# A fused conditioning and mixture-of-experts kernel on one core: the order of VectorE's work in the first group, and of TensorE's products and VectorE's weighing in the second

## The chip, the cores and the metric

The kernel runs on one core of a Trainium2 chip. The metric is the device time of one execution in microseconds (us), and less is better. Beside each timed execution one was profiled: its trace gives every instruction's start and length on TensorE (PE for the products, PEld for the loads of the stationary operand), VectorE (DVE), ScalarE (ACT), GpSimd (POOL) and the queue of SyncE (SP), which issues most transfers.

## What is computed

The reference, cut to what matters (64 batches of 64 rows, so 4096 rows of 512; 6 experts of rank 16):

```python
q_emb = relu(cond @ W3 + b3)
x1 = (64 * x + sum(x, axis=1)) * q_emb[:, None, :]
y = relu(x1 @ W2 + b2)
gates = softmax(y @ W_router + b_router)
w = the gates of the two best experts, zero elsewhere
h = y @ A_r            # per expert, and y @ A_s shared
out = x + y @ W_base + b_base + (y @ A_s) @ B_s + sum_e (w_e * h_e) @ B_r[e]
```

Each float32 factor is split into a rounded part (`hi`) and a rest (`lo`), and a product is three products of TensorE: hi with hi, hi with lo, lo with hi.

## The kernel before

The 4096 rows are eight groups of 512 tokens. A group's work has these parts:

- **x.** The four pieces `c` of 128 features come transposed. VectorE turns a piece (`turn_x`, `turn`), sums it per batch and adds (`sum_x` and `add_sum`, together `total`), GpSimd scales it by `qT` (`scale`, L308), ScalarE rounds it to `x1_hi` (`x1_split`, L347, in the step called `split`), and VectorE takes the rest `x1_lo` (`x1_rest`, L491, in the step called `rest`). The pieces of group g + 1 are made while group g is multiplied.
- **m1.** y's four tiles `m` of 128 features, each a sum over the four pieces: 12 products a tile, 48 in all. Tiles 0, 1 and 2 have PSUM banks of their own. Tile 3 has the bank of `m2_ps[2]`, so it begins only when VectorE has read the output tile 2 of the group before (`add_x`, L625).
- **relu.** For each tile ScalarE writes `y_hi` (L353), and then the full value back to the bank (L355). VectorE takes the rest `y_lo` (`y_rest`, L497).
- **h and m2.** 12 products of y with the narrow weights give `hT` (`h`), and 48 with `W_base` give the output tiles (`m2`).
- **Routing.** ScalarE copies `hT` to `h_head` (L441), VectorE ranks the experts and makes the gates (L544 to L583, `rank_experts` and `gates`), and SP spreads the gates to `gatesT` by four DMAs (L263). In the next group's step VectorE weighs h (`weigh`, L598), ScalarE rounds it (`hw_split`, L415), VectorE takes its rest (`hw_rest`, L611), and TensorE adds 12 products to the output tiles that stand in PSUM (`up`, in the order 2, 0, 1, 3). Then `add_x` adds x to each tile and SP stores it.

There is no scheduler. Each engine runs a list written out by hand, in its own order, and waits on semaphores. TensorE's order in a group but the first is: m1 of tiles 0 to 2, `up` for the group before, m1 of tile 3, three of the four parts of `h`, six products of `m2`, the last part of `h`, and the other 42 products of `m2`. That is 120 products a group. The wait ahead of m1 of tile 3 is this line, and `UP_TILES[:1]` is output tile 2:

```python
if m == KC - 1:
    pe.wait_ge(out_ready, TT * (g - 1) + 1)
```

The first group differs. Its x is turned by TensorE (`head_ps`), `h` and `m2` of output tile 0 alternate, and there is no `up`. The second group's step on VectorE is the branch `elif second`, and the products of its m1 are in the loop `m1(g, par, m)`, tile by tile, with a wait for `x1_lo` of piece k ahead of the three products of piece k. Products with zeros (`keep_warm`, L724) fill TensorE's time at the start. VectorE's time, for the x of group g + 1 and for y of group g, is one queue, so whatever stands ahead of an instruction there delays it.

Of the kernel before, what the change touches and what calls it, by code (L numbers as in the profile page):

```python
# [22 lines left out]
def adaln_ffn(nc, x, cond, W3, b3, W2, b2, W_base, b_base, A_s, B_s, A_r, B_r, W_router, b_router, out):  # L23
# [6 lines left out]
    P = 128  # L30
# [3 lines left out]
    KC = D // P  # L34
    QC = Q // P
    TG = 512
# [11 lines left out]

    WARM_LOAD, WARM_W3, WARM_HALF, WARM_Q = 7, 1, 2, 1
    assert ONE < SH and SH + R <= RO and RO + E * R == P and TT == KC and NG % 2 == 0 and NG >= 4  # L50
# [6 lines left out]
    with ctx:  # L57
# [277 lines left out]
        def _(act):  # L335
# [43 lines left out]

            q_relu(0)  # L380
            W2_split(0)
            q_relu(1)
            x1_split_head(0)
            q_relu(2)
            x1_split_head(1)
            q_relu(3)
            W2_split(1)
# [31 lines left out]
            def step(g, par):  # L419
                first, second, last = place(g)  # L420

                def split(c):
                    if not last:
                        x1_split(g + 1, 1 - par, c)

                for m in range(KC):
                    relu(g, m, first)
                    if m == 0 and not first:
                        hw_split(slice(0, TG), g)
                    if not first and m >= (2 if second else 1):  # L430
                        split(m - (2 if second else 1))
                if first:
                    act.wait_ge(Wu_loaded, 48)
                    nc.scalar.activation(Wu_hi[:, :], Wu_f[:, :], ACT.Copy).then_inc(Wu_hi_ready, 1)
                    pick_round()

# [8 lines left out]
                if first:  # L445
                    split(0)
                    split(1)
# [16 lines left out]
        def _(dve):  # L464
# [163 lines left out]
            def step(g, par):  # L628
# [20 lines left out]

                if first:  # L650
                    turn(0)
                    total(0)
                    y_rest(g, 0)
                    turn(1)
                    y_rest(g, 1)
                    sum_x(g + 1, 1)
                    y_rest(g, 2)
                    add_sum(g + 1, 1)
                    y_rest(g, 3)
                    turn(2)  # L660
                    total(2)
                elif second:
                    y_rest(g, 0)
                    weigh_before()
                    turn(0)
                    total(0)
                    hw_rest_before()
                    y_rest(g, 1)
# [31 lines left out]
                if first:  # L700
                    rest(0)
                if first or second:
                    turn(3)
                    total(3)
                if first:
                    rest(1)
                rest(2)
# [12 lines left out]
        def _(pe):  # L720
# [50 lines left out]
            def m1_first():  # L771
# [5 lines left out]

                for k in range(KC // 2):
                    pe.wait_ge(x1_hi_ready, k + 1)
                    pe.wait_ge(W2_hi_ready, k + 1)  # L780
                    for m in range(KC):
                        if k == 0:
                            pe.wait_ge(qT_ready, m + 1)
                        chunk(m, k, W2_hi, x1_hi)
                    pe.wait_ge(W2_lo_ready, k + 1)
                    for m in range(KC):
                        chunk(m, k, W2_lo, x1_hi)
                    pe.wait_ge(x1_lo_ready, k + 1)
                    for m in range(KC):
                        chunk(m, k, W2_hi, x1_lo)  # L790
                for tiles in ((0, 1), (2, 3)):
                    for k in range(KC // 2, KC):
                        pe.wait_ge(x1_hi_ready, k + 1)
                        pe.wait_ge(W2_lo_ready, k + 1)
                        for m in tiles:
# [4 lines left out]
                            if k == KC - 1:  # L800
                                last.then_inc(m1_done, 1)

            def h(g, k, first):
# [52 lines left out]
            def step(g, par):  # L856
                first, second, last = place(g)
                if first:
                    m1_first()
                else:  # L860
                    for m in range(KC - 1):
                        m1(g, par, m)
                    up(UP_TILES, g)
                    m1(g, par, KC - 1)
# [57 lines left out]
```

## Time and profile before

| what | value |
|---|---|
| time, median of 3 runs | 237.69 us (237.68 to 237.79) |
| time of the profiled execution | 237.04 us |
| its span, first to last instruction | 235.2 us |
| TensorE busy with products | 229.3 us (97%), 1006 products |
| VectorE busy | 166.7 us (71%) |
| ScalarE busy | 86.2 us (37%) |
| GpSimd busy | 49.0 us (21%) |

A product's record lasts 0.39 us, but the records overlap: products are pipelined, so it is the distance from one start to the next that counts. A start that comes later than that distance after the start ahead of it is time that TensorE stood still.

### The profile page before, as it was taken

Reading aid. Unit: us, or ns where it says so; the run is one execution under the profiler, and the core shown is the slowest. Engines: PE = TensorE matmul, PEld = TensorE weight load, DVE = VectorE, ACT = ScalarE, POOL = GpSimd, SP = SyncE. Lnnn points to the kernel's source line nnn. Section 1 sums busy time; section 2 is a strip of 40 time slices with the busy share of each in tenths; the row PEclk is TensorE's granted clock in tenths of the full one; section 3 lists DMA queues with packets and bytes.
Section 4 is the critical chain, followed back from the end, with each engine's and each line's share of the span. In section 5 each row is a group of like instructions: output and inputs, shape, how many; then the busy total and the mean of one; then the engine's idle time right before and its main releaser. Section 6 shows DMA issues by size and latency. Waiting matters only on the chain.

```text
span 235.2 us, 3088 instructions
## 1 busy us (share of the span) xinstructions
PE 229.3 (97%) x1006; PEld 186.9 (79%) x1006; DVE 166.7 (71%) x309; ACT 86.2 (37%) x171; POOL 49.0 (21%) x57
## 2 busy tenths in 40 slices
PE   7999899999999999999999999999999999999994
PEld 3977687788888888888888888888888888888883
DVE  0794997798979967497838969299665976064344
ACT  3369451534136330444206340263305351252330
POOL 6288422012132211023012120022111130000000
PEclk9999999999999999999999999999999999999999
DMA  6999903527053632717044541709020370104004
GB/s 214 340 219 227 253 4 71 142 99 261 11 137 65 222 137 37 175 70 289 8 117 89 187 172 22 185 4 329 28 33 0 126 231 13 22 0 178 3 0 178
DMA packets 32505, 28.80 MB, mean 122 GB/s; under 512 B 5817, under 2 KB 22909, under 8 KB 32494
## 3 DMA queue, kind: packets, MB, share of 16 engines
q1 hardware_dynamic: 30682, 28.50, 42.4%
q10 hardware_dynamic: 1812, 0.17, 0.6%
q8 instruction: 6, 0.10, 0.2%
q14 instruction: 5, 0.04, 0.1%
HBM read 18.89 MB, written 8.39 MB: 116 GB/s over the span
## 4 chain that ended last, share of the span: by engine, by line
PE 87%; SPq 6%; DVE 2%; DMA 2%; issue 0%; DVEq 0%
PE m_ps L747 78%; PE hT L747 9%; SPq L210 3%; DMA x_quart<-in_x_dram 2%; DVE out_nat L625 1%; SPq L226 1%; SPq L233 1%; SPq L229 1%; DVE xT L471 0%; SPq L231 0%; DVE vsum L476 0%; DVE x_sum L483 0%; SPq L237 0%; DVE y_lo L497 0%; SPq L236 0%
## 5 line engine op out<-in xcount | busy, mean ns | idle before, releaser
L308 POOL TENSOR_TENSOR x_full<-x_sum,qT 128x512 f32<-128x512 f32 x28 | 32.4, 1156 | 136.7 <-DVE x_sum L483 136.7
L353 ACT ACTIVATE y_hi<-m_ps,condT 128x512 fp32r<-128x512 f32 x32 | 21.9, 686 | 80.4 <-PE m_ps L747 80.2
L747 PE MATMUL m_ps<-Wb_lo,y_hi 128*128 128x512 f32 x128 | 49.8, 389 | 0.0
L747 PE MATMUL m_ps<-Wb_hi,y_hi 128*128 128x512 f32 x128 | 49.8, 389 | 0.0
L747 PE MATMUL m_ps<-Wb_hi,y_lo 128*128 128x512 f32 x128 | 49.8, 389 | 0.0
L747 PE MATMUL m_ps<-x_hi,W_hi 128*128 128x512 f32 x112 | 43.8, 391 | 0.0
L747 PE MATMUL m_ps<-x_hi,W_lo 128*128 128x512 f32 x112 | 43.6, 389 | 0.0
L747 PE MATMUL m_ps<-x_lo,W_hi 128*128 128x512 f32 x112 | 43.6, 389 | 0.0
L497 DVE TENSOR_TENSOR y_lo<-m_ps,y_hi 128x512 fp32r<-128x512 f32 x32 | 21.7, 677 | 30.3 <-ACT m_ps L355 30.3
L471 DVE STREAM_TRANSPOSE xT<-x_quart 128x512 f32<-128x512 f32 x28 | 30.3, 1084 | 3.0 <-DMA x_quart<-in_x_dram 3.0
L747 PEld LDWEIGHTS m_ps<-Wb_hi,y_lo 128*128 128x128 f32 x128 | 24.0, 188 | 5.0
L747 PEld LDWEIGHTS m_ps<-Wb_hi,y_hi 128*128 128x128 f32 x128 | 24.0, 188 | 4.9
L747 PEld LDWEIGHTS m_ps<-Wb_lo,y_hi 128*128 128x128 f32 x128 | 24.0, 188 | 4.9
L747 PEld LDWEIGHTS m_ps<-x_hi,W_hi 128*128 128x128 f32 x112 | 21.0, 188 | 5.0 <-DVE x_lo L491 0.7
L747 PEld LDWEIGHTS m_ps<-x_hi,W_lo 128*128 128x128 f32 x112 | 21.0, 188 | 4.4
L747 PEld LDWEIGHTS m_ps<-x_lo,W_hi 128*128 128x128 f32 x112 | 21.0, 188 | 4.2
L347 ACT ACTIVATE x_hi<-x_full 128x512 fp32r<-128x512 f32 x28 | 17.5, 628 | 17.7 <-POOL x_full L308 17.7
L625 DVE TENSOR_TENSOR out_nat<-m_ps,x_nat 128x512 f32<-128x512 f32 x32 | 20.4, 679 | 2.1 <-PE m_ps L747 2.1
L491 DVE TENSOR_TENSOR x_lo<-x_full,x_hi 128x512 fp32r<-128x512 f32 x28 | 19.3, 707 | 2.5 <-ACT x_hi L347 2.4
L355 ACT ACTIVATE m_ps<-m_ps,condT 128x512 f32<-128x512 f32 x32 | 20.9, 653 | 0.0
L483 DVE SCALAR_TENSOR_TENSOR x_sum<-xT,vsum 128x512 f32<-128x512 f32 x28 | 19.4, 692 | 2.1
L476 DVE TENSOR_REDUCE vsum<-xT 128x8 f32<-128x512 f32 x28 | 19.0, 680 | 0.4
(99 smaller groups left out, 255.1 us busy)
## 6 DMA issues: line engine op xcount, KB each, us to landing
out_dram<-out_nat SPq DMA_DIRECT2D x32, 256.0 KB, 2.3
x_quart<-in_x_dram SPq DMA_DIRECT2D x28, 256.0 KB, 4.5
x_nat<-in_x_dram SPq DMA_DIRECT2D x7, 1024.0 KB, 6.2
gatesT<-wT SPq DMA_DIRECT2D x28, 48.0 KB
x_nat<-in_x_dram SPq DMA_DIRECT2D x4, 256.0 KB, 3.4
W_f<-in_L_cond_W_dram SPq DMA_DIRECT2D x4, 256.0 KB, 6.0
Wb_f<-in_L_ffn_W_base_dram SPq DMA_DIRECT2D x1, 1024.0 KB, 8.7
W_sb<-in_L_cond_W_dram SPq DMA_DIRECT2D x2, 256.0 KB, 4.2
```

The costliest lines, as they stand in the source:

```text
L210: eng.dma_start(Wd_f[:, k, RO:P].rearrange("p (e r) -> p e r", r=R), A_r[:, k * P:(k + 1) * P, :].rearrange("e p r -> p e r")).then_inc(Wd ...
L308: nc.gpsimd.tensor_tensor(per_batch(x1_full[:, c, :]), per_batch(x1_sum[:, c, :]), qT[:, c, bass.ds(BG * g, BG)].unsqueeze(2).to_broadcast ...
L347: nc.scalar.activation(x1_hi[par][:, c, :], x1_full[:, c, :], ACT.Copy).then_inc(x1_hi_ready, 1)
L353: nc.scalar.activation(y_hi[:, m, :], m1_ps[m][:, :], ACT.Relu, bias=b2_sb[:, m:m + 1]).then_inc(y_hi_ready, 1)
L355: nc.scalar.activation(m1_ps[m][:, :], m1_ps[m][:, :], ACT.Relu, bias=b2_sb[:, m:m + 1]).then_inc(y_full_ready, 1)
L471: nc.vector.transpose(xT[c % 2][:, :], x_quart[par][:, :, :].rearrange("p b (i c) -> p c b i", c=KC)[:, c]).then_inc(xT_ready, 1)
L476: nc.vector.tensor_reduce(vsum[c % 2][:, :], per_batch(xT[c % 2][:, :]), AX.X, ALU.add).then_inc(vsum_ready, 1)
L483: nc.vector.scalar_tensor_tensor(out=per_batch(x1_sum[:, c, :]), in0=per_batch(xT[c % 2][:, :]), scalar=float(N), in1=vsum[c % 2][:, :].un ...
L491: nc.vector.tensor_tensor(x1_lo[par][:, c, :], x1_full[:, c, :], x1_hi[par][:, c, :].bitcast(F32), ALU.subtract).then_inc(x1_lo_ready, 1)
L497: nc.vector.tensor_tensor(y_lo[:, m, :], m1_ps[m][:, :], y_hi[:, m, :].bitcast(F32), ALU.subtract).then_inc(y_lo_ready, 1)
L625: nc.vector.tensor_tensor(out_nat[par][:, t, :], m2_ps[t][:, :], x_nat[par][:, t, :], ALU.add).then_inc(out_ready, 1)
L747: mm = nc.tensor.matmul(psum, lhsT, rhs, start=start and i == 0, stop=stop and i == len(terms) - 1)
```

## The change

Four places are edited. The values and the number of instructions are the same, but for one product with zeros less.

1. **Head.** `WARM_HALF` goes from 2 to 1. ScalarE rounds each `q_relu` one place earlier. In the first group's m1, piece 0, tile 3's two products with `x1_hi` go behind those of tiles 0 to 2, so that the wait for the last `qT` comes later.
2. **First group, VectorE.** Each `y_rest` goes ahead of the piece of x that stood before it. `turn(2)` and `total(2)` go behind the gates, and the first `rest` behind `total(3)`. ScalarE takes `split(0)` ahead of the copy of `hT`, and the four copies called `pick_round` go to the second group.
3. **Second group, TensorE.** m1 of tiles 0 to 2 takes the 24 products with `x1_hi`, piece by piece over the three tiles, and then the 12 with `x1_lo`, tile by tile (`m1_second`).
4. **Second group, VectorE and ScalarE.** `weigh` and `hw_rest` go ahead of all `y_rest`, and `hw_split` ahead of all `relu`.

```diff
-    WARM_LOAD, WARM_W3, WARM_HALF, WARM_Q = 7, 1, 2, 1
+    WARM_LOAD, WARM_W3, WARM_HALF, WARM_Q = 7, 1, 1, 1
...
             q_relu(0)
+            q_relu(1)
             W2_split(0)
-            q_relu(1)
+            q_relu(2)
             x1_split_head(0)
-            q_relu(2)
+            q_relu(3)
             x1_split_head(1)
-            q_relu(3)
             W2_split(1)
...
+                if second:
+                    hw_split(slice(0, TG), g)
                 for m in range(KC):
                     relu(g, m, first)
-                    if m == 0 and not first:
+                    if m == 0 and not first and not second:
                         hw_split(slice(0, TG), g)
...
                     nc.scalar.activation(Wu_hi[:, :], Wu_f[:, :], ACT.Copy).then_inc(Wu_hi_ready, 1)
+                    split(0)
+                if second:
                     pick_round()
...
                 if first:
-                    split(0)
                     split(1)
...
                 if first:
+                    y_rest(g, 0)
+                    turn(0)
+                    y_rest(g, 1)
+                    total(0)
+                    y_rest(g, 2)
+                    turn(1)
+                    y_rest(g, 3)
+                    total(1)
+                elif second:
+                    weigh_before()
+                    hw_rest_before()
+                    y_rest(g, 0)
                     turn(0)
                     total(0)
...
-                elif second:
-                    y_rest(g, 0)
-                    weigh_before()
-                    turn(0)
-                    total(0)
-                    hw_rest_before()
                     y_rest(g, 1)
                     turn(1)
                     add_x(g - 1, 1 - par, UP_TILES[:1], 0)
...
                 if first:
-                    rest(0)
+                    turn(2)
+                    total(2)
                 if first or second:
                     turn(3)
                     total(3)
                 if first:
+                    rest(0)
                     rest(1)
...
+            def m1_second():
+
+                x_hi, x_lo = x1_hi[1], x1_lo[1]
+                for k in range(KC):
+                    pe.wait_ge(x1_hi_ready, KC + k + 1)
+                    for m in range(KC - 1):
+                        cols = slice(m * P, (m + 1) * P)
+                        product(m1_ps[m][:, :], [(W2_hi[:, k, cols], x_hi[:, k, :]),
+                                                 (W2_lo[:, k, cols], x_hi[:, k, :])], k == 0, False)
+                for m in range(KC - 1):
+                    cols = slice(m * P, (m + 1) * P)
+                    for k in range(KC):
+                        if m == 0:
+                            pe.wait_ge(x1_lo_ready, KC + k + 1)
+                        mm = product(m1_ps[m][:, :], [(W2_hi[:, k, cols], x_lo[:, k, :])], False, k == KC - 1)
+                    mm.then_inc(m1_done, 1)
...
-                    for m in range(KC - 1):
+                    if second:
+                        m1_second()
+                    for m in () if second else range(KC - 1):
                         m1(g, par, m)
```

The first place is VectorE from the last rest of the head to the ranking, in the first group. `xT`, `vsum` and `x_sum` belong to the x of the second group, `y_lo` to the y of the first. Before:

```order
L523 TENSOR_TENSOR x_lo<-hT,x_hi 128x512
L471 STREAM_TRANSPOSE xT<-x_quart 128x512
L476 TENSOR_REDUCE vsum<-xT 128x8
L483 SCALAR_TENSOR_TENSOR x_sum<-xT,vsum 128x512
L497 TENSOR_TENSOR y_lo<-m_ps,y_hi 128x512
L471 STREAM_TRANSPOSE xT<-x_quart 128x512
L497 TENSOR_TENSOR y_lo<-m_ps,y_hi 128x512
L476 TENSOR_REDUCE vsum<-xT 128x8
L497 TENSOR_TENSOR y_lo<-m_ps,y_hi 128x512
L483 SCALAR_TENSOR_TENSOR x_sum<-xT,vsum 128x512
L497 TENSOR_TENSOR y_lo<-m_ps,y_hi 128x512
```

The same stretch of VectorE in the changed kernel:

```order
L526 TENSOR_TENSOR x_lo<-hT,x_hi 128x512
L500 TENSOR_TENSOR y_lo<-m_ps,y_hi 128x512
L474 STREAM_TRANSPOSE xT<-x_quart 128x512
L500 TENSOR_TENSOR y_lo<-m_ps,y_hi 128x512
L479 TENSOR_REDUCE vsum<-xT 128x8
L486 SCALAR_TENSOR_TENSOR x_sum<-xT,vsum 128x512
L500 TENSOR_TENSOR y_lo<-m_ps,y_hi 128x512
L474 STREAM_TRANSPOSE xT<-x_quart 128x512
L500 TENSOR_TENSOR y_lo<-m_ps,y_hi 128x512
L479 TENSOR_REDUCE vsum<-xT 128x8
L486 SCALAR_TENSOR_TENSOR x_sum<-xT,vsum 128x512
```

The first `y_lo` moved ahead of three instructions on x, and the last one from behind two turns and a whole sum to behind two turns and the first piece's sum.

The second place is the second group: TensorE's products of m1, with buffer numbers. Before, from the last three of tile 0 (`m1_ps0`) to the first of tile 1:

```order
L747 MATMUL m1_ps0<-x1_hi1,W2_hi 128x512
L747 MATMUL m1_ps0<-x1_lo1,W2_hi 128x512
L747 MATMUL m1_ps0<-x1_hi1,W2_lo 128x512
L747 MATMUL m1_ps1<-x1_hi1,W2_hi 128x512
L747 MATMUL m1_ps1<-x1_lo1,W2_hi 128x512
```

The same place of TensorE in the changed kernel, the last piece's products with `x1_hi` and all with `x1_lo`, up to the first product of `up` (`Wu_hi`):

```order
L749 MATMUL m1_ps0<-x1_hi1,W2_hi 128x512
L749 MATMUL m1_ps0<-x1_hi1,W2_lo 128x512
L749 MATMUL m1_ps1<-x1_hi1,W2_hi 128x512
L749 MATMUL m1_ps1<-x1_hi1,W2_lo 128x512
L749 MATMUL m1_ps2<-x1_hi1,W2_hi 128x512
L749 MATMUL m1_ps2<-x1_hi1,W2_lo 128x512
L749 MATMUL m1_ps0<-x1_lo1,W2_hi 128x512 x4
L749 MATMUL m1_ps1<-x1_lo1,W2_hi 128x512 x4
L749 MATMUL m1_ps2<-x1_lo1,W2_hi 128x512 x4
L749 MATMUL m2_ps2<-Wu_hi,hw_hi 128x512
```

Tile 0's last product was the 12th of the group, and is now the 28th; tile 1's went from the 24th to the 32nd, and tile 2's stays the 36th. `up` follows as the 37th in both.

VectorE in the same group, from the first `y_lo` to the first addition of x (`out_nat`), before:

```order
L497 TENSOR_TENSOR y_lo<-m_ps,y_hi 128x512
L598 SCALAR_TENSOR_TENSOR hw_full<-hT,h_bias,gatesT 128x512
L471 STREAM_TRANSPOSE xT<-x_quart 128x512
L476 TENSOR_REDUCE vsum<-xT 128x8
L483 SCALAR_TENSOR_TENSOR x_sum<-xT,vsum 128x512
L611 TENSOR_TENSOR hw_lo<-hw_full,hw_hi 128x512
L497 TENSOR_TENSOR y_lo<-m_ps,y_hi 128x512
L471 STREAM_TRANSPOSE xT<-x_quart 128x512
L625 TENSOR_TENSOR out_nat<-m_ps,x_nat 128x512
```

And in the changed kernel:

```order
L601 SCALAR_TENSOR_TENSOR hw_full<-hT,h_bias,gatesT 128x512
L614 TENSOR_TENSOR hw_lo<-hw_full,hw_hi 128x512
L500 TENSOR_TENSOR y_lo<-m_ps,y_hi 128x512
L474 STREAM_TRANSPOSE xT<-x_quart 128x512
L479 TENSOR_REDUCE vsum<-xT 128x8
L486 SCALAR_TENSOR_TENSOR x_sum<-xT,vsum 128x512
L500 TENSOR_TENSOR y_lo<-m_ps,y_hi 128x512
L474 STREAM_TRANSPOSE xT<-x_quart 128x512
L628 TENSOR_TENSOR out_nat<-m_ps,x_nat 128x512
```

`hw_full` and `hw_lo` left the stretch between the first `y_lo` and `out_nat` and stand ahead of it; the first `y_lo`, the first piece of x, the second `y_lo` and a turn still stand ahead of `out_nat`.

The third place is ScalarE in the head, the difference between the two (`qT` is `q_relu`, `W_hi` is `W2_split`, `x_hi` is `x1_split_head`):

```order
-L367 ACTIVATE qT<-m_ps,b_sb 128x64
+L367 ACTIVATE qT<-m_ps,b_sb 128x64 x2
 L373 ACTIVATE W_hi<-W_f 128x512
 L367 ACTIVATE qT<-m_ps,b_sb 128x64
```

Two `qT` now stand ahead of the first `W_hi`, and so three ahead of the first `x_hi`, where there were two.

## Rows read from the trace of the kernel before

**Rows 1.** The page: TensorE's granted clock in 40 slices, tenths of full speed.

```profile
PEclk9999999999999999999999999999999999999999
```

**Rows 2.** Chain that ended last, one later group: start, length (us), what.

```profile
83.49 23.12 PE m_ps L747 x102
```

**Rows 3.** Timeline of the head: start, length, what, idle before.

```profile
8.52 0.59 PE L724 MATMUL m_ps<-idle 128*128 128x512 bf16 x2
8.95 1.40 PE L766 MATMUL m_ps<-condT,W_sb 128*128 128x64 f32 x6
...
9.52 0.31 ACT L367 ACTIVATE qT<-m_ps,b_sb 128x64 f32<-128x64 f32 x1 [4.09 <-PE m_ps L766]
9.73 0.62 ACT L373 ACTIVATE W_hi<-W_f 128x512 fp32r<-128x512 f32 x1
...
10.26 0.31 ACT L367 ACTIVATE qT<-m_ps,b_sb 128x64 f32<-128x64 f32 x1
...
10.60 0.60 ACT L378 ACTIVATE x_hi<-m_ps 128x512 fp32r<-128x512 f32 x1
...
11.25 1.43 PE L774 MATMUL m_ps<-x_hi,W_hi 128*128 128x512 f32 x4
...
17.43 0.19 PEld L774 LDWEIGHTS m_ps<-x_lo,W_hi 128*128 128x128 f32 x1 [0.17 <-DVE x_lo L523]
```

**Rows 4.** Timeline of the first group: y of it, x of the second.

```profile
20.02 0.65 ACT L355 ACTIVATE m_ps<-m_ps,condT 128x512 f32<-128x512 f32 x1
...
21.15 1.10 DVE L471 STREAM_TRANSPOSE xT<-x_quart 128x512 f32<-128x512 f32 x1 [3.01 <-DMA x_quart<-in_x_dram]
...
22.55 0.39 PE L747 MATMUL hT<-y_hi,Wd_hi 128*128 128x512 f32 x1
...
23.62 0.68 DVE L497 TENSOR_TENSOR y_lo<-m_ps,y_hi 128x512 fp32r<-128x512 f32 x1
...
24.22 1.10 DVE L471 STREAM_TRANSPOSE xT<-x_quart 128x512 f32<-128x512 f32 x1
24.36 0.50 PE L747 MATMUL hT<-y_lo,Wd_hi 128*128 128x512 f32 x1 [1.19 <-DVE y_lo L497]
29.23 1.50 ACT L441 ACTIVATE h_head<-hT,h_bias 32x128 f32<-32x128 f32 x4 [3.05 <-PE hT L747]
```

**Rows 5.** Timeline of the second group: TensorE, ScalarE and GpSimd.

```profile
37.33 1.43 POOL L308 TENSOR_TENSOR x_full<-x_sum,qT 128x512 f32<-128x512 f32 x1 [5.46 <-DVE x_sum L483]
...
37.87 0.39 PE L747 MATMUL m_ps<-x_hi,W_hi 128*128 128x512 f32 x1
38.78 0.63 ACT L347 ACTIVATE x_hi<-x_full 128x512 fp32r<-128x512 f32 x1 [6.10 <-POOL x_full L308]
40.76 0.40 PE L747 MATMUL m_ps<-x_hi,W_lo 128*128 128x512 f32 x1
41.20 0.69 ACT L353 ACTIVATE y_hi<-m_ps,condT 128x512 fp32r<-128x512 f32 x1 [1.78 <-PE m_ps L747]
41.78 0.65 ACT L355 ACTIVATE m_ps<-m_ps,condT 128x512 f32<-128x512 f32 x1
49.33 0.39 PE L747 MATMUL m_ps<-x_hi,W_hi 128*128 128x512 f32 x1
```

**Rows 6.** Timeline of the second group: VectorE, and SP's issues of `gatesT`.

```profile
34.26 3.88 SPq L263 DMA_DIRECT2D gatesT<-wT  x4
42.47 0.69 DVE L497 TENSOR_TENSOR y_lo<-m_ps,y_hi 128x512 fp32r<-128x512 f32 x1 [2.33 <-ACT m_ps L355]
43.08 0.74 DVE L598 SCALAR_TENSOR_TENSOR hw_full<-hT,h_bias,gatesT 128x512 f32<-128x512 f32 x1
43.73 1.09 DVE L471 STREAM_TRANSPOSE xT<-x_quart 128x512 f32<-128x512 f32 x1
...
46.19 0.68 DVE L611 TENSOR_TENSOR hw_lo<-hw_full,hw_hi 128x512 fp32r<-128x512 f32 x1
...
48.41 0.65 DVE L625 TENSOR_TENSOR out_nat<-m_ps,x_nat 128x512 f32<-128x512 f32 x1
```

More of the change, by code:

```diff
@@ L650, in step @@
                 if first:
+                    y_rest(g, 0)
[10 more added lines that the diff above has]
+                    y_rest(g, 0)
                     turn(0)
                     total(0)
-                    y_rest(g, 0)
[L654 to L661, printed above, removed]
-                elif second:
-                    y_rest(g, 0)
-                    weigh_before()
-                    turn(0)
-                    total(0)
-                    hw_rest_before()
                     y_rest(g, 1)
@@ L776, in chunk @@
                                             stop=k == KC - 1 and x1 is x1_lo)
-                for k in range(KC // 2):
+                pe.wait_ge(x1_hi_ready, 1)
+                pe.wait_ge(W2_hi_ready, 1)
+                for m in range(KC - 1):
+                    pe.wait_ge(qT_ready, m + 1)
+                    chunk(m, 0, W2_hi, x1_hi)
+                pe.wait_ge(W2_lo_ready, 1)
+                for m in range(KC - 1):
+                    chunk(m, 0, W2_lo, x1_hi)
+                pe.wait_ge(qT_ready, KC)
+                chunk(KC - 1, 0, W2_hi, x1_hi)
+                chunk(KC - 1, 0, W2_lo, x1_hi)
+                pe.wait_ge(x1_lo_ready, 1)
+                for m in range(KC):
+                    chunk(m, 0, W2_hi, x1_lo)
+                for k in range(1, KC // 2):
                     pe.wait_ge(x1_hi_ready, k + 1)
@@ L781, in m1_first @@
                     for m in range(KC):
-                        if k == 0:
-                            pe.wait_ge(qT_ready, m + 1)
                         chunk(m, k, W2_hi, x1_hi)
@@ L801, in m1_first @@
                                 last.then_inc(m1_done, 1)
+            def m1_second():
+                x_hi, x_lo = x1_hi[1], x1_lo[1]
+                for k in range(KC):
+                    pe.wait_ge(x1_hi_ready, KC + k + 1)
+                    for m in range(KC - 1):
+                        cols = slice(m * P, (m + 1) * P)
+                        product(m1_ps[m][:, :], [(W2_hi[:, k, cols], x_hi[:, k, :]),
+                                                 (W2_lo[:, k, cols], x_hi[:, k, :])], k == 0, False)
+                for m in range(KC - 1):
+                    cols = slice(m * P, (m + 1) * P)
[4 more added lines that the diff above has]
+                    mm.then_inc(m1_done, 1)
             def h(g, k, first):
```

## The prediction

> **What bounds the kernel now.** I read the page first: TensorE is busy 97% of the span, at full clock in every slice [rows 1]. So the time is TensorE's products at their distance, plus the places where it stands still. The chain that ended last gives the distance: 102 products in 23.12 us, 0.227 us each [rows 2]. With it I went through TensorE's timeline. From 42 us to the end each start follows the last by that distance, so nothing on another engine costs time there. The still times are all ahead of 50 us, and the change works on them:
>
> - In the first group `h` starts at 22.55, and its third product should start at 23.00. It starts at 24.36, because VectorE turned and summed a piece of x from 21.15 on and reached the first `y_lo` only at 23.62 [rows 4]. With restarts after short waits, the 60 products from 22.55 to 37.87 take 15.32 us, where 60 distances are 13.60: 1.72 us lost [rows 4, 5].
> - In the second group, from 37.87 to the start of m1's tile 3 at 49.33, 48 products take 11.46 us, where 48 distances are 10.88: 0.58 us lost, in short waits for `x_lo` and `hw_lo` [rows 5].
>
> These 2.3 us are what the change can win. To know what it wins I walk the new order with the lengths of the old rows.
>
> **Part by part: the head.** One product with zeros less lets the last `q` products start 0.21 us earlier (two took 0.59 us, and one record is 0.38) [rows 3]. The first `q_relu` moves from 9.52 to 9.31. The second tile's sum follows the first: six products in 1.40 us, the last one 0.40 long, are 0.20 apart, two for a tile, so the second `q_relu` starts at 9.71. Then comes `W2_split` 0.21 later (as 9.52 to 9.73), at 9.92, the third `q_relu` 0.53 later (as 9.73 to 10.26), at 10.45, and the first `x_hi` 0.21 to 0.34 later (9.52 to 9.73, 10.26 to 10.60), at 10.66 to 10.79, where it was 10.60 [rows 3]. I take 10.70: the first product of m1 0.1 us later than before. The later wait for `qT` gives TensorE 0.25 us back: its first four products took 0.93 us from start to start where 0.34 + 2 x 0.23 = 0.80 would do, and it restarted once more for 0.11 us. But at 17.43 TensorE waited for an `x_lo` [rows 3]. That one ends an unbroken line of work on VectorE, which starts from the first `x_hi`, and so comes 0.1 us later too. **Head: +0.1 us.** Its ends are -0.2 (all of the 0.21 kept) and +0.3 (the `x_hi` at 10.79, and 0.1 for another wait).
>
> **First group.** `h` starts at 22.65. The first full y is there at 20.02 + 0.1 + 0.65 = 20.77 [rows 4], when VectorE still waits for the x transfer (to 21.15), so the first `y_lo` takes time that was idle: 20.8 to 21.5. After it VectorE runs without a break: `y_lo` 0.60 to its successor (23.62 to 24.22), a turn 1.0, `y_lo` 0.60, sum and addition 1.33 (43.73 to 46.19 is 2.46 with the turn's 1.13), `y_lo` 0.60, a turn 1.0, and the fourth `y_lo` 0.68 [rows 4, 6]. It ends at 26.65. TensorE wants it for the 21st product, at 22.65 + 20 x 0.227 = 27.18, and the others with more to spare. So the 60 products run at their distance, and the second group starts at 22.65 + 13.60 = **36.25 us, 1.62 earlier than 37.87**.
>
> **Second group, m1 and x.** Is its x there? `hT` is complete 1.62 earlier, so its copy starts at 27.61 instead of 29.23 [rows 4]. From that copy to SP's first issue of `gatesT` were 5.03 us (29.23 to 34.26) [rows 4, 6]; as much at most gives 32.65. Two turns and sums follow (2 x 2.46), to 37.6, then GpSimd's scaling (1.43) and ScalarE's rounding (0.63) [rows 5]: the fourth `x_hi` is there at 39.75 with 0.1 for the handing over. Before it was there at 39.41, and so this is about as late as it was, but the new order wants it only at the 19th product, 36.25 + 18 x 0.227 = 40.33. The fourth `x_lo` is there at 40.5, and wanted by the 28th, at 42.37. No wait is left, with 0.6 us to spare. The weighing now stands ahead of `y_lo` on VectorE and could block it: SP's four issues end 1.6 earlier, at 36.5, and `weigh` at 43.08 did not wait for a landing 4.9 us behind its last issue at 38.14 [rows 6], so the gates are there by 41.5 at the latest. 0.74 + 0.63 + 0.68 for `hw_full`, `hw_hi` and `hw_lo` end by 43.7, ahead of `up` (36.25 + 36 x 0.227 = 44.41) and of the first full y. **The 0.58 us are won too: -2.2 us by the end of `up`,** at 36.25 + 10.88 = 47.13.
>
> **What is late next.** m1 of tile 3 needs its bank, which VectorE frees by the first `out_nat`. Before, that ended at 48.41 + 0.65 = 49.06, and TensorE came at 49.33 [rows 5, 6]: 0.27 us ahead. It stands behind the second group's first `y_lo`, a turn, a sum, the second `y_lo` and another turn. The first `y_lo` needs tile 0 of m1 complete, and by `m1_second` that is no longer the 12th product but the 28th. It starts at 42.37. Then ScalarE: `y_hi` 0.44 later (40.76 to 41.20), L355 another 0.58 (41.20 to 41.78), 0.65 long [rows 5]: 44.04, and VectorE's `y_lo` at 44.08. Before it started at 42.47 [rows 6]. **So it comes 1.6 us later, though m1 starts 1.6 us earlier.** From its start to the end of `out_nat` were 6.59 us (42.47 to 49.06). `hw_full` and `hw_lo` leave that stretch: 0.65 (43.08 to 43.73) and 0.60 less [rows 6], 5.34 us. `out_nat` ends at 49.42. TensorE's load starts 0.06 later (24.30 to 24.36), at 49.48, and a restart costs 0.1 (the record of 24.36 is 0.50 long, not 0.39) [rows 4]: as if at 49.58. Before: 49.33.
>
> **Sum.** -1.62 (first group, with the head's +0.1 in it), -0.58 (second group's waits), +2.45 (a new wait of 2.35 us, and a restart), together **+0.25 us**. All later work on TensorE moves by that; VectorE's line, 0.36 later at `out_nat`, reaches the x of the third group before it is wanted. The profiled execution's 237.04 us become 237.3. It was 0.65 under the median of the runs, so 237.69 becomes **237.9 us**. What the first edits save is saved on TensorE ahead of a point whose time VectorE sets. Each tenth that m1 of the second group starts sooner still moves that point, since the chain hangs on its start; the order of the products costs 16 x 0.227 = 3.6 us on it.
>
> **Rivals.**
>
> - *The saving is kept* (6 in 100). If m1 of tile 3 did not wait, everything would move by -1.62 - 0.58 = -2.2: 235.5 us. For it speaks that two operations of VectorE leave the stretch, 1.25 us; against it that 0.27 us was all there was to spare, and that 1.6 + 2.2 us are to be made up. A shorter line on VectorE, by 0.7 us, would already be faster by over 0.2%: 2 in 100.
> - *Slower: VectorE's line to `out_nat` is longer than I sum it.* I have +0.25, and +0.48 is the bound of 0.2%, so 0.23 us decide. The head's +0.3 instead of +0.1 gives 238.1; a late piece of x in the second group, past its 0.6 us to spare, or `hw_lo` in front of the first `y_lo`, past 0.3, adds what it is late by. Two such tenths give 238.3 to 238.5. 14 in 100.
> - *Slower: the clock.* TensorE would stand still for 2.35 us, longer than the 1.2 us at 24.36, through which the clock stayed at full [rows 1, 4]. If it fell to the lower of its two levels, half of the upper, the twelve products of tile 3 would take 0.227 us more each: +2.7, 240.6 us. The Trainium skill ("TensorE: Matmul & The Clock Gate", Part 1: The HAM clock gate) says that the throttled state is the default and that activity releases it, which speaks for such a fall; the trace shows none after any still time of before. 4 in 100.
>
> **How the numbers follow.** 0.2%, 0.48 us, is about what a measurement of this kernel can tell from no change. My forecast, the saving given back at m1 of tile 3, has the rest, 74 in 100. Its own bounds are the head's (-0.3 to +0.2 about my value), the chain's (0.1 either way) and the spread of the runs (0.1): 237.5 to 238.3. With the slower line the range is 237.4 to 238.5, and leaves out the kept saving, the clock and the ends of the rest, under 2 in 10. Faster 8 in 100, within 0.2% 74, slower 18.
>
> **What would show it.** Right: no wait of TensorE for `y_lo` in the first group; the second group's first product near 36.3; no waits in its m1; then a wait of TensorE for `out_nat` of 2.3 us near 47.1 to 49.5, which the trace of before has nowhere; the first `y_lo` of the second group near 44.1. Wrong in the head: the first `x_hi` at 10.5 or earlier, or after 10.8. It would be wrong as a whole if m1 of tile 3 starts near 47.2, if a clock below 1.00 stands behind the wait, or if TensorE waits again after 52 us.

## The result, and the profile after

| | before | changed |
|---|---|---|
| median of 6 runs | 237.69 us (236.98 to 237.79) | 240.64 us (238.99 to 242.09) |
| ratio to before, 95% interval | | 1.0129 (1.0081 to 1.0177) |
| granted clock of the executions, mean | 0.997 to 1.000 in all 91 timed beside the later experiments | 0.993 in two, 0.986 in four |
| profiled execution: time, span | 237.04, 235.2 us | 242.09, 240.1 us |

The kernel became 2.95 us slower, outside the range of 237.4 to 238.5 us. Its times are also spread over 3 us, where before they lay within 1. The page of the changed kernel shows two slices in which TensorE was granted less than its full clock, where before there was none [rows 1]:

```profile
span 240.1 us, 3086 instructions
PEclk9979999997999999999999999999999999999999
```

The view of TensorE's loads and whom they waited for has the forecast wait, and no wait for `y_lo` or for the second group's `x_lo` any more (columns: us in total, times, longest):

```profile
PEld m_ps L749 <- DVE out_nat L628: 2.6, 1, 2.6
...
PEld m_ps L776 <- ACT x_hi L378: 0.3, 1, 0.3
```

The timeline of the same execution: the first product of the head's m1, and then from `h` of the first group to m1's tile 3 of the second. It answers to [rows 3 to 6]:

```profile
13.25 1.65 PE L776 MATMUL m_ps<-x_hi,W_hi 128*128 128x512 f32 x3
...
25.68 0.39 PE L749 MATMUL hT<-y_hi,Wd_hi 128*128 128x512 f32 x1
...
26.13 0.39 PE L749 MATMUL hT<-y_lo,Wd_hi 128*128 128x512 f32 x1
...
39.28 0.39 PE L749 MATMUL m_ps<-x_hi,W_hi 128*128 128x512 f32 x1
...
44.72 2.88 PE L749 MATMUL m_ps<-x_lo,W_hi 128*128 128x512 f32 x12
...
45.83 0.69 ACT L353 ACTIVATE y_hi<-m_ps,condT 128x512 fp32r<-128x512 f32 x1 [0.66 <-PE m_ps L749]
...
47.10 0.69 DVE L500 TENSOR_TENSOR y_lo<-m_ps,y_hi 128x512 fp32r<-128x512 f32 x1 [1.20 <-ACT m_ps L355]
...
51.75 0.65 DVE L628 TENSOR_TENSOR out_nat<-m_ps,x_nat 128x512 f32<-128x512 f32 x1
...
52.45 0.50 PE L749 MATMUL m_ps<-x_hi,W_hi 128*128 128x512 f32 x1 [2.14 <-DVE out_nat L628]
...
53.98 0.63 PE L749 MATMUL m_ps<-x_hi,W_hi 128*128 128x512 f32 x1
...
56.55 0.63 PE L749 MATMUL hT<-y_hi,Wd_hi 128*128 128x512 f32 x1
```

Three things are to be seen. From `h` to the second group the 60 products take 13.60 us (25.68 to 39.28), their distance and nothing more. m1's tile 3 starts 13.17 us after m1 itself, where the walk had 13.23. And both stand 3.1 us late: `h` starts at 25.68, where before it was 22.55 [rows 4]. The head lost that, and in two places: its first product of m1 starts 2.0 us later than before (13.25, before 11.25 [rows 3]), and from there to `h` are 12.43 us, where before they were 11.30. Behind the wait the products' records grow from 0.39 to 0.63 us and their distance from 0.227 to 0.43.

The windows view gives the granted clock of such stretches, the number behind the five engines' busy times. The windows of 1 us show how low it goes, the longer ones its surroundings:

```profile
12.50:15.00 2.50, 2.35 (x7) 1.91 (x7) 2.15 (x4) 2.47 (x7) 1.73 (x2) 0.59 1.21 188
13.00:14.00 1.00, 0.85 (x3) 0.66 (x3) 0.77 (x2) 1.00 (x4) 0.85 (x1) 0.50 1.39 193
15.00:20.00 5.00, 5.00 (x20) 4.02 (x20) 4.68 (x8) 2.82 (x6) 4.62 (x4) 0.86 1.08 223
...
48.00:52.00 4.00, 2.32 (x11) 1.58 (x9) 3.93 (x6) 1.79 (x4) 1.04 (x1) 1.00 0.00 0
52.00:56.00 4.00, 3.54 (x11) 2.86 (x12) 3.97 (x7) 0.21 (x1) 0.00 (x0) 0.74 0.33 126
54.00:55.00 1.00, 1.00 (x4) 0.81 (x3) 1.00 (x3) 0.00 (x0) 0.00 (x0) 0.50 0.33 127
56.00:60.00 4.00, 4.00 (x16) 3.17 (x16) 2.65 (x5) 2.89 (x7) 1.25 (x1) 0.84 0.95 309
```

The clock is lower twice: in the head, when the first group's m1 has just begun, and behind the wait. In both it goes to 0.50, the lower of its two levels, 1.2 instead of 2.4 GHz. Ahead of the first fall TensorE did narrow products of `q` with one product with zeros less among them, ahead of the second it stood still. From 53.72 to 57.37 nine distances take 3.65 us, where 9 x 0.227 are 2.04: that fall cost 1.6 us. The other fall is the 1.1 us that the way to `h` grew by.

A third stretch is not in the clock row. The head's transposes of x, before any edit takes effect, ran at two speeds. The view of the tile `hT`, from 4 to 10 us, lists its four transposes (shortest, median, longest in ns, first and last start); in the changed kernel's profile:

```profile
L739 PE MATMUL hT<-ident,x_nat x4: 421/421/421, 6.0 to 8.6; 128*128 128x128 f32 x4
```

In the profile of before:

```profile
L737 PE MATMUL hT<-ident,x_nat x4: 283/283/284, 5.5 to 6.9; 128*128 128x128 f32 x4
```

So the profile of before, on which the walk was built, had a quick head, and this one a slow head from its first products on. Whether that is of the change had to be asked too. A start like the one of before, with the first `q` product at 7.28 us, is called an early start below; in this profile it comes at 9.24, a late start.

### The profile page after: what moved, and what is told of

Same layout as the page of the kernel before. It is cut to its first block, busy times and chain, and to the rows that moved or that the text cites. A ratio compares the mean times of both kernels' runs of the same rounds, so it can differ in the third digit from the quotient of the medians.

```text
span 240.1 us, 3086 instructions
## 1 busy us (share of the span) xinstructions
PE 233.0 (97%) x1005; PEld 191.1 (80%) x1005; DVE 166.2 (69%) x309; ACT 86.4 (36%) x171; POOL 48.8 (20%) x57
## 4 chain that ended last, share of the span: by engine, by line
PE 94%; DVE 2%; DMA 1%; ACT 1%; issue 1%; ACTq 0%; DVEq 0%
PE m_ps L749 77%; PE hT L749 9%; PE m_ps L776 5%; DMA cond_sb<-in_L_cond_b_dram 1%; DVE out_nat L628 1%; PE m_ps L739 1%; PE m_ps L768 1%; DVE xT L474 0%; PE hT L739 0%; PE m_ps L726 0%; ACTq L336 0%; ACT qT L367 0%; ACT W_hi L373 0%; ACT x_hi L378 0%; PE m_ps L732 0%
## 5 line engine op out<-in xcount | busy, mean ns | idle before, releaser
L749 PE MATMUL m_ps<-x_hi,W_lo 128*128 128x512 f32 x112 | 44.1, 394 | 0.0
L749 PE MATMUL m_ps<-x_lo,W_hi 128*128 128x512 f32 x112 | 42.3, 393 | 0.0
```

The source lines that it names most:

```text
L749: mm = nc.tensor.matmul(psum, lhsT, rhs, start=start and i == 0, stop=stop and i == len(terms) - 1)
```

## The experiments

All were timed over 5 rounds beside the kernel before. "Clock" is the mean granted clock of an execution, listed for each. One low stretch makes 0.993 (or 0.990 to 0.992) of it, two make 0.986.

**e1: the product with zeros back.**

```diff
-    WARM_LOAD, WARM_W3, WARM_HALF, WARM_Q = 7, 1, 1, 1
+    WARM_LOAD, WARM_W3, WARM_HALF, WARM_Q = 7, 1, 2, 1
```

> The changed kernel with WARM_HALF back at 2, all else as changed. Theory A (the low clock of the head, 13.0 to 16.4 us, comes of the product with zeros that was taken out): only the low clock behind the wait for out_nat is left in every execution, mean granted clock 0.993, 238.9 to 239.6 us. Theory B (it comes of the other edits of the head, or of a chance in how early the clock rises at the start): 0.986 in about as many executions as in the changed kernel, 4 in 6, and the median stays near 240.6 us.

Measured: 239.30 us (237.42 to 240.04, 9 runs), ratio 1.0057 (1.0037 to 1.0078). No execution at 0.986: four at 0.993 (239.30 to 240.04) and five at 1.000 (237.42 to 239.31). Theory A holds for the head: the execution with two low stretches is gone. It was wrong in one thing, that the fall behind the wait comes in every execution: it comes in four of nine. The profiled execution is one without it, with an early start, and so the one that the prediction walked through. Its timeline:

```profile
36.49 0.39 PE L749 MATMUL m_ps<-x_hi,W_hi 128*128 128x512 f32 x1
...
44.31 0.69 DVE L500 TENSOR_TENSOR y_lo<-m_ps,y_hi 128x512 fp32r<-128x512 f32 x1 [1.19 <-ACT m_ps L355]
...
48.97 0.65 DVE L628 TENSOR_TENSOR out_nat<-m_ps,x_nat 128x512 f32<-128x512 f32 x1
...
49.67 0.50 PE L749 MATMUL m_ps<-x_hi,W_hi 128*128 128x512 f32 x1 [2.14 <-DVE out_nat L628]
```

Forecast were 36.25, 44.08, an end of `out_nat` at 49.42 (here 49.62) and 49.48. The execution took 237.42 us, and 237.3 was forecast for one like the profile of before.

**e2: the head's edits alone, on the kernel before** (`WARM_HALF` 1, the order of `q_relu`, the order of piece 0 in the first group's m1).

> The kernel before with the edits of the head alone (WARM_HALF 1, ScalarE's and TensorE's new order). Theory A: the low clock of the head is there in some executions, 0.993 in those, 1.000 in the others, and the time is bimodal, 237.7 and about 239.3 us. Rival (the head is innocent, both low stretches belong to the groups): 1.000 always and 237.5 to 237.9 us.

Measured: 237.81 us (237.31 to 238.46, 12 runs), ratio 1.0002 (0.9993 to 1.0012). The clock is 0.990 or 0.993 in ten of twelve executions, and between 0.997 and 1.000 in all 32 of the kernel before beside them. So the head's edits make the clock fall, and the time doesn't move: neither expectation had that. Executions at 0.993 average 237.73 us, the two without a fall 238.00. In the profiled one the clock is low from 12 to 14 us, and `h` starts 1.7 us later than in the profile of before. The low clock has 0.9 us of that (from the first product of m1 to `h` are 12.23 us, where 11.30 were), and a later start the rest:

```profile
12.00:14.00 2.00, 1.96 (x5) 1.58 (x6) 1.95 (x3) 1.80 (x4) 1.30 (x2) 0.50 1.14 347
```

```profile
L747 PE MATMUL hT<-y_hi,Wd_hi x4: 389/392/395, 24.3 to 29.3; 128*128 128x512 f32 x4
L747 PE MATMUL hT<-y_lo,Wd_hi x4: 389/444/502, 25.3 to 29.8; 128*128 128x512 f32 x4
```

The first `y_lo` product follows at 25.3, where before it was 24.36. Of 1.7 us of lateness 0.8 was hidden in the wait for `y_lo` here.

**e3: the changed kernel, with ten products with zeros in the wait for `out_nat`.**

```diff
                     up(UP_TILES, g)
+                    if second:
+                        for _ in range(10):
+                            nc.tensor.matmul(hT[:, :], idle[:, 0:P], idle[:, :], start=True, stop=True)
```

> The changed kernel with ten products with zeros on TensorE (into the bank of hT, which is free there) ahead of the wait for out_nat in the second group. The wait stays, 2.3 us, but TensorE is at work in it. Theory (the clock falls because TensorE stands still there, and that costs 1.7 us on top of the wait): no low clock at 54 to 57 us, and the time is 1.5 to 1.7 us less than the changed kernel's, 237.9 us where the head keeps its clock and 239.3 to 240.4 where it doesn't. Rival (the low clock has another cause, or the wait alone costs the time): no gain, 240.6 us.

Measured: 239.00 us (237.66 to 240.42, 12 runs), ratio 1.0050 (1.0031 to 1.0069), 1.6 us less than the changed kernel. The lowest clock is 0.992, in five of twelve: the second fall is gone. The two ranges that were expected, with and without the head's fall, are not what came. The seven without it lie at 237.66 to 238.03 (three) and 239.10 to 239.41 (four), the five with it at 238.56 to 239.06 and once at 240.42. So there are two heaps 1.4 us apart, and the head's fall adds about 1 us to either. The waits of its loads have 0.5 us left for `out_nat`:

```profile
PEld m_ps L749 <- DVE out_nat L628: 0.5, 1, 0.5
```

The windows behind it are at full clock, where the head's 12 to 14 us are not:

```profile
12.00:14.00 2.00, 2.00 (x6) 1.52 (x6) 1.86 (x4) 1.42 (x3) 1.30 (x2) 0.50 1.18 324
...
54.00:56.00 2.00, 2.00 (x10) 1.66 (x9) 1.67 (x3) 1.09 (x3) 1.25 (x1) 1.00 1.01 379
```

**e4: `add_x` of output tile 2 early.** VectorE's order in the second group of the changed kernel:

```diff
                     weigh_before()
+                    turn(0)
                     hw_rest_before()
+                    total(0)
                     y_rest(g, 0)
-                    turn(0)
-                    total(0)
                     y_rest(g, 1)
-                    turn(1)
                     add_x(g - 1, 1 - par, UP_TILES[:1], 0)
+                    turn(1)
```

> The changed kernel with VectorE's order in the second group weigh, turn(0), hw_rest, total(0), y_rest 0, y_rest 1, add_x of output tile 2, turn(1). Theory (VectorE's line to out_nat gives the saving back): TensorE waits no more ahead of m1 of tile 3, no low clock behind it, and 237.69 - 2.2 = 235.5 us where the head keeps its clock, 237.0 to 238.0 where it doesn't. Rival (the wait is set by something else, as the products of up or a late piece of x): a wait of over 1 us stays, and over 238 us.

Measured: 237.12 us (235.64 to 238.18, 12 runs), ratio 0.9982 (0.9959 to 1.0004). The wait for `out_nat` is gone from TensorE's waits. The clock is 0.990 or 0.993 in nine of twelve; that this is the head's fall is shown by e5, not by this run's profile, which has none. 3.5 us less than the changed kernel, and that includes the fall behind the wait. Without it the profiles give 2.2 us: from the second group's m1 to the end are 197.0 us here and 199.2 in e1. So the line on VectorE is what gave the saving back. The edit shortens that line in two ways, which were not separated: `turn(1)` leaves it, and `turn(0)` and `total(0)` go ahead of the first `y_rest`.

**e5: e4 with `WARM_HALF` 2.**

> As e4, with WARM_HALF back at 2. Theory A (the low clock of the head comes of the product taken out, and each us that the head is late is now a us of the kernel): no low clock anywhere, 235.5 us where the clock rises early at the start and about 236.9 where it rises late; median under 236.5, below e4's 237.12. Theory B (the spread of e4 has another cause): as e4, 237.1 us.

Measured: 236.28 us (235.61 to 237.19, 7 runs), ratio 0.9946 (0.9922 to 0.9969). All executions at 0.998 to 1.000, as theory A had it. The times lie in two heaps, 235.61 to 236.28 (four) and 237.06 to 237.19 (three). VectorE's `out_nat` ends at 47.68 in its profile, and TensorE starts tile 3 at 48.29 without a wait:

```profile
23.81 0.39 PE L749 MATMUL hT<-y_hi,Wd_hi 128*128 128x512 f32 x1
...
47.00 0.68 DVE L628 TENSOR_TENSOR out_nat<-m_ps,x_nat 128x512 f32<-128x512 f32 x1
...
48.29 0.39 PE L749 MATMUL m_ps<-x_hi,W_hi 128*128 128x512 f32 x1
```

**e6: the first group's edits alone, on the kernel before.**

> The kernel before with the first group's edits alone (each y_rest ahead, turn(2) and total(2) behind the gates, ScalarE's split(0) ahead and pick_round in the second group). Theory: h runs without a wait, and m1 of the second group starts 1.6 us earlier, but tile by tile it wants x_lo of the fourth piece at its 12th product, 38.6 us, and has it at 40.4: the saving goes into that wait. 237.5 to 237.9 us, more where the clock falls behind it. Rival (the first group's saving is kept without the second group's edits): 236.1 us.

Measured: 238.83 us (238.11 to 240.20, 8 runs), ratio 1.0051 (1.0029 to 1.0073). Slower than either expectation. The saving does go into waits for `x_lo`, two of them, the first of 2.1 us already at the first piece, since its `rest` now stands behind `total(3)`:

```profile
39.94 0.47 PE L747 MATMUL m_ps<-x_hi,W_hi 128*128 128x512 f32 x1 [1.92 <-DVE x_lo L492]
...
41.30 0.50 PE L747 MATMUL m_ps<-x_hi,W_hi 128*128 128x512 f32 x1 [0.43 <-DVE x_lo L492]
```

One of the eight executions is at 0.992. So each half of the change needs the other: this one needs `m1_second`, which asks for `x_lo` late.

**e7: the second group's edits alone, on the kernel before.**

> The kernel before with the second group's edits alone (m1_second, weigh and hw_rest ahead of y_rest, hw_split ahead of relu). Theory (tile 0 done 16 products later sets out_nat): m1 starts at 37.9 as before, out_nat ends 1.6 us later, a wait of 2.3 us; 239.5 us where the clock keeps its level, 240.9 to 241.2 where it falls behind the wait. Rival (the wait costs only what the first group's edits saved): 237.7 us.

Measured: 239.55 us (239.44 to 241.58, 6 runs), ratio 1.0106 (1.0073 to 1.0139). Four executions at 1.000, 239.44 to 239.60, and two at 0.993, 241.26 and 241.58. The sizes are about as the theory had them: +1.9 us for tile 0 done 16 products later, and 1.9 more where the clock falls behind the wait, of which 1.4 to 1.7 were expected. The timeline:

```profile
46.42 0.69 DVE L499 TENSOR_TENSOR y_lo<-m_ps,y_hi 128x512 fp32r<-128x512 f32 x1 [1.99 <-ACT m_ps L355]
...
51.08 0.64 DVE L627 TENSOR_TENSOR out_nat<-m_ps,x_nat 128x512 f32<-128x512 f32 x1
...
51.78 0.50 PE L749 MATMUL m_ps<-x_hi,W_hi 128*128 128x512 f32 x1 [2.14 <-DVE out_nat L627]
```

**e8 and e9: the same lateness put into two kernels,** the kernel before (e8) and e5 (e9): six products with zeros more behind the first `q` products, 1.27 us.

```diff
-                keep_warm(WARM_HALF if k == 0 else WARM_Q)
+                keep_warm(WARM_HALF + 6 if k == 0 else WARM_Q)
```

> The kernel before with six products with zeros more in the head, behind the first q products: all of the head 1.27 us later. Theory (the x transfer and the pieces of x, not TensorE, set the third product of h there, so a late head is hidden in its wait): under 0.3 us on the median, 237.7 to 238.0 us. Rival (the head is on the path): 239.0 us.

> e5 with the same six products with zeros more in the head as e8. Theory (with each y_rest ahead, the first group's h waits for nothing, and a late head is a late kernel): the full 1.27 us on e5's 236.28, 237.3 to 237.8 us, where the same edit cost the kernel before 0.4 us. Rival (the head is hidden here too): under 236.8 us.

Measured: e8 238.10 us (237.56 to 238.39, 12 runs), ratio 1.0010 (0.9999 to 1.0021), +0.4 us, a little over the 0.3 expected. e9 238.19 us (236.92 to 238.70, 12 runs), ratio 0.9999 (0.9979 to 1.0020). Its median is 1.9 us over e5's, more than the 1.27 us put in, but both kernels have two heaps, and the median changed heaps. Heap by heap, the means went from 235.91 (four of e5) to 237.17 (five of e9) and from 237.13 (three) to 238.41 (seven): +1.26 and +1.28 us, the lateness put in and nothing else. So before, two thirds of such lateness are hidden, and in the new order of the first group nothing is. e8's profile, which has the late start as well, shows how the kernel before hides it. VectorE's head ends at 21.33, and the turn of x follows at 21.25, 0.1 us later than before [rows 4]; `h` starts at 25.73, 3.2 us later than before, and its `y_lo` product at 26.18 without a wait:

```profile
20.64 0.69 DVE L523 TENSOR_TENSOR x_lo<-hT,x_hi 128x512 fp32r<-128x512 f32 x1
21.25 1.12 DVE L471 STREAM_TRANSPOSE xT<-x_quart 128x512 f32<-128x512 f32 x1
...
24.24 0.68 DVE L497 TENSOR_TENSOR y_lo<-m_ps,y_hi 128x512 fp32r<-128x512 f32 x1
...
25.73 0.39 PE L747 MATMUL hT<-y_hi,Wd_hi 128*128 128x512 f32 x1
...
26.18 0.39 PE L747 MATMUL hT<-y_lo,Wd_hi 128*128 128x512 f32 x1
```

That execution's span is 236.3 us, 1.1 more than that of before, for 3.2 us of lateness.

**e10: e5 with an eighth product with zeros at the start** (`WARM_LOAD` 8).

> e5 with an eighth product with zeros ahead of the transposes. Theory (the records' two speeds of the transposes, 0.28 and 0.42 us each, are the clock's rise at the start, which falls early or late): if more work in front makes the early rise more frequent, the median goes from 236.28 towards 235.7 and the spread shrinks. Rival (the time of the rise is not set by it): 236.3 to 236.5 us, spread as before.

Measured: 236.31 us (235.87 to 236.61, 6 runs), ratio 0.9927 (0.9902 to 0.9952). The spread shrank to 0.74 us and the median did not move: the first as the theory had it, the second as its rival. In its profile the transposes of `hT` have both lengths (283/309/418 ns, shortest, median, longest), so if the two lengths are two levels of the clock, the rise fell among them.

**e11: e3 with `WARM_HALF` 2,** so both causes of a low clock are gone and the wait is left.

> The changed kernel with both causes of low clock taken away: WARM_HALF 2 and the ten products in the wait for out_nat. Theory (what is left is the saving given back at out_nat, plus the late start where the clock rises late): clock 1.000 in every execution, 237.4 us with an early rise and about 238.8 with a late one. Rival (there is a further loss): a low clock or over 239.2 us.

Measured: 239.14 us (238.18 to 239.51, 11 runs), ratio 1.0041 (1.0022 to 1.0060), all executions at 0.999 or 1.000. The times are in two heaps, 238.18 to 238.51 (five) and 239.14 to 239.51 (six). The lower heap is 0.9 us above the 237.4 expected. Its profiled execution (238.37 us) shows why: it has the quick transposes, but among them TensorE waited 0.2 us for the last of x's four transfers. Its first `q` product starts at 7.86 where e1's starts at 7.36, and `h` at 23.58 where e1's is at 22.89. So a start can be late in two ways. In e5's profile this wait is the longest:

```profile
7.35 0.63 PE L739 MATMUL m_ps<-ident,x_nat 128*128 128x128 f32 x3 [0.50 <-DMA x_nat<-in_x_dram]
```

That the upper heap is the slow transposes is likely, but not shown: it wants a profile of each execution.

**e12: e5 with the whole head of before.**

> e5 with the head of before altogether, ScalarE's and TensorE's order too. Theory of the prediction (the new order of the head costs 0.1 us at the first x_hi): 0.1 us less than e5, 235.9 to 236.4 us. Rival (the later wait for the last qT gives TensorE 0.25 us back): 0.2 us or more above e5.

Measured: 236.26 us (235.27 to 237.92, 12 runs), ratio 0.9932 (0.9910 to 0.9954). 0.02 us from e5. The medians tell neither the 0.1 us of the prediction nor its rival's 0.2 from nothing, but the profiles do. From the first `q` product to the first product of m1 are 3.97 us with the head of before (before, e7, e12), 4.22 with the new order (e1, e10), and 4.00 with the new order and the product with zeros taken out (e4). In some others the first six `q` products take 0.2 us more, and the way is longer by that. From there to `h` all have 11.3. So the new order costs 0.25 us, and the product's absence gives 0.2 of it back.

**e13: the changed kernel again,** beside e14.

> The changed kernel unaltered, with the clock of every execution. Theory (two low clocks, each in a share of the executions, of some 1.5 us each): executions with 0.986, 0.993 and perhaps 1.000, each level 1.2 to 1.8 us above the next; median 240.0 to 241.0 us. Rival (the low clock of the head costs nothing, or one of the two is worth nearly all): no step between 0.993 and 0.986.

Measured: 240.82 us (239.10 to 242.01, 6 runs), ratio 1.0131 (1.0097 to 1.0165). One execution at 1.000 (239.10), three at 0.993 (240.18 to 240.83), two at 0.986 (241.75 and 242.01). With the six of the result: one, five and six of twelve, at 239.10, 240.18 (median, 238.99 to 240.83) and 241.75 us (median, 240.54 to 242.09). The steps are 1.1 and 1.6 us, but they don't tell the price of each fall. The level 1.000 is a single execution, one at 0.993 is below it (238.99), and 0.993 can be either fall, with either start. In this run's profile, at 0.993, the clock falls behind the wait, and the head from 12 to 18 us is at full clock:

```profile
52.00:54.00 2.00, 2.00 (x6) 1.54 (x6) 2.00 (x4) 0.00 (x0) 0.00 (x0) 0.50 0.25 91
```

What each fall costs stands in the profiles, below.

**e14: e4's order, the whole head of before, `WARM_LOAD` 8.**

> The first group's and second group's edits with add_x early (as e4), the whole head of before, and eight products with zeros at the start. Theory (no wait for out_nat, no low clock, and the eighth product narrows the late start): 1.000 in all, 235.8 to 236.4 us, spread under 1 us, as e10. Rival (e10's narrow spread was chance): 235.3 to 238 us as e12.

Measured: 236.10 us (235.10 to 236.66, 6 runs), ratio 0.9929 (0.9912 to 0.9947). All at 0.999 or 1.000. The spread is 1.6 us, so e10's 0.74 was partly chance. This, e10 and e12 are the fastest versions, 1.5 to 1.6 us under the kernel before, and are not told apart.

## Why the prediction was wrong

**Right, with its size.** The saving is given back at m1 of tile 3, by the mechanism and at the place that were named. TensorE's idle time there was put at 2.35 us, and 49.93 + 0.23 to 52.45 is 2.3. The walk from the start of m1 to tile 3 was 13.23 us, and the changed kernel took 13.17, e1 13.18. No wait in `h`, none in the second group's m1, `weigh` not late. Making VectorE's line shorter turned the loss into a gain of 1.4 us (e5). The wait without any low clock is 2.2 us in the profiles (199.2 us from the second group's m1 to the end in e1 and e11, 197.0 in e5); it was summed as 2.45.

**Wrong: "TensorE would stand still for 2.35 us", with 4 in 100 for a fall of the clock.** The clock did fall behind that wait. The price was named, 2.7 us, and is 1.6 (nine distances in the profile; and 200.8 us from the second group's m1 to the end, where e1 has 199.2) to 1.9 (e7's two heaps), since the clock fell only when half of tile 3's twelve products were done, and rose with the second product of `h`. The chance was wrong by far. The prediction took the unmoved clock after 1.2 us of standing still [rows 4] as evidence for 2.35. The fall comes in 4 of 9 executions of e1, in 2 of 6 of e7, and in at least seven of twelve of the changed kernel's, the six at 0.986 and e13's profile; filled with products, it is gone (e3, e11). The rule that was cited beside it, that the throttled state is the default and activity releases it (the Trainium skill, "TensorE: Matmul & The Clock Gate", Part 1: The HAM clock gate), was the better guide, and the trace of the changed kernel agrees with it: 0.74 in the window behind the wait. That the rival's 240.6 us is the measured 240.64 is luck: its price was 1.1 us too high, and terms that it did not have made up for it.

**Wrong: "One product with zeros less lets the last `q` products start 0.21 us earlier".** That was all that the walk made of the product. It had a second use. Without it the clock falls in the head in 10 of 12 executions (e2), and in 9 of 12 of e4; with it in none of e5's 7 and of e11's 11. No rival had this. All these have the head's new order; the product taken out of the old head alone was not run. The product costs 0.21 us and saves a stretch at half clock, which costs 0.9 to 1.1: from the first product of m1 to `h` are 11.3 us in the thirteen profiles without that stretch, and 12.2 to 12.4 in the three with it (e2, e3, the changed kernel's).

**Wrong: "Head: +0.1 us", and "It was 0.65 under the median of the runs, so 237.69 becomes 237.9".** The head's own term was right (0.04 us, below). But it was added to the start of one profiled execution, and the distance to the median was carried over as if it were a constant. In the sixteen profiles the first `q` product starts between 7.28 and 9.35 us, and the profile of before is the earliest of them. Seven have transposes at 0.42 us, and their first `q` product starts at 8.9 or later, `h` at 24.2 or later. In others the transposes are quick and an x transfer landed late (e2, e5, e11). Before, all that hardly shows: VectorE turned and summed x ahead of the first `y_lo`, from 21.15 on, when the transfer had landed, and `h` waited 1.2 us for it. A head late by that much, or by a low clock, disappeared in the wait (e2: 0.1 us on the median for a low clock in ten of twelve; e8: 0.4 us for 1.27). The change takes the wait out, which is its gain of 1.7 us, and with it the cover. So the gain is only had when the head is on time, and all that is late counts in full (e9).

**The sum as the profiles give it,** in us (each row is the time from the event of the row above it):

| part | before | changed | e1 | e13 | e5 | e8 |
|---|---|---|---|---|---|---|
| start to the first `q` product | 7.28 | 9.24 | 7.36 | 9.12 | 8.15 | 9.17 |
| to the first product of m1 | 3.97 | 4.01 | 4.22 | 4.17 | 4.35 | 5.27 |
| to `h` | 11.30 | 12.43 | 11.31 | 11.29 | 11.31 | 11.29 |
| to the second group's m1 | 15.32 | 13.60 | 13.60 | 13.60 | 13.60 | 13.60 |
| to the end | 197.3 | 200.8 | 199.2 | 200.8 | 197.0 | 197.0 |
| span | 235.2 | 240.1 | 235.7 | 239.0 | 234.4 | 236.3 |

The three terms that the prediction added up were right: +0.04 for the head, -1.72 for the first group, and +1.9 for the second (199.2 less 197.3), together +0.2 us, where +0.25 was forecast. The changed kernel's profile is 4.9 us longer than that of before, and the other 4.7 are three terms that the sum put at nothing: a start 1.96 later that nothing hides any more, 1.1 for the low clock in the head, and 1.6 for the one behind the wait.

On the medians the same three are mixed. The executions of e1, e3 and e11 at full clock lie at 237.42 to 238.51 (twelve), about the forecast range, and at 239.10 to 239.51 (eleven). How many of a run fall in which heap moves its median by up to 1.4 us: the upper one has one of e1's five, four of e3's seven and six of e11's eleven. So e11, with both low clocks gone, is not below e1 (239.30) and e3 (239.00), and the differences of these medians don't price the terms one by one. How much of the median's 2.95 us is the start and how much the clock stays open.

## What to carry to other kernels

A wait that is taken out was perhaps the cover of something else's spread: before a saving is booked, look how late the work ahead of it may come in other executions, not only in the one that was profiled. One profile can be the earliest of all, as here, and medians of a kernel with two heaps of times can move without a cause: compare heap with heap. Reordering a product so that its first result comes last moves every bank that waits for that result; walk the line from the new time to the next bank that TensorE needs. And on TensorE a stretch of standing still, or a product with zeros less between narrow products, has a second price in the clock, which the order of instructions doesn't show: time such an edit by itself, and read the granted clock of each execution.

## What the runs showed of the hardware

- The clock's fall is a matter of chance per execution at the same instructions: 4 of 9 (e1), 10 of 12 (e2), 2 of 6 (e7). One low stretch cost 0.9 to 1.1 us in the head and 1.6 to 1.9 behind the wait.
- The granted clock reads 1.00 in the first 10 us in both profiles above, while the same transposes take 0.28 us in one and 0.42 in the other, and the first seven products with zeros are 0.43 us apart in both. The two lengths suggest the two levels of the clock; the clock row does not show it, so for the start of a program the records' lengths are the better evidence. Which of the two a start gets varied among profiles of kernels whose first 8 us are the same. The x transfers' landing varied too: the wait for one among the transposes was 0.5 us in e5, 0.2 in e2 and e11, and none in before and e1.
- Ten products with zeros, on a bank that nobody needs just then, kept the clock up through the wait of 2.3 us: none of the 23 executions of e3 and e11 had two low stretches, and those of e11 had none.
